# Feed-forward stage, first batch: statistics and normalising of the next x tile by tile over seven steps, turning and copies a step later

## The reference

```python
x = x + tanh(g_xattn) * cross_attention(layernorm(x), ctx)      # x: 16 batches of 512 x 512, f32
h = layernorm(x) @ W1 + b1                                      # 512 -> 2048
imag = w_imag * sin(phases + 0.1 * h)
q = h + (cos(phases) * w_real + sin(phases) * w_imag) * imag * 0.1
x = x + tanh(g_ffn) * (relu(q) @ W2 + b2)                       # 2048 -> 512
```

## Time and profile before

| | |
|---|---|
| median of 3 runs | 2136.64 us (2135.77 to 2136.66) |
| the profiled execution's own time | 2137.62 us |
| its span | 2135.8 us |
| PE busy | 2112.7 us (99%) |
| DVE, ACT, POOL busy | 1436.0 (67%), 1163.2 (54%), 398.5 us (19%) |
| mean granted TensorE clock | 0.998 |

### The profile page before, as it was taken

The page is one execution under the profiler, slowest core; times in us unless marked ns, Lnnn a source line. Parts: engine busy times, 40 slices in busy tenths (PEclk is TensorE's granted clock), DMA queues, the critical chain, the costliest instruction groups (busy, mean ns, idle before and its releaser), DMA issues.

```text
span 2135.8 us, 29046 instructions
## 1 busy us (share of the span) xinstructions
PE 2112.7 (99%) x10331; PEld 1709.8 (80%) x10331; DVE 1436.0 (67%) x2457; ACT 1163.2 (54%) x3463; POOL 398.5 (19%) x324
## 2 busy tenths in 40 slices
PE   9999999999999999999999999999999999999999
PEld 7777777777777778888888888888888888888887
DVE  5587778778776587666665666656666666566654
ACT  3487777777777465444444444444454444544443
POOL 3043443344443311010110100101101011010110
PEclk9999999999999999999999999999999999999999
DMA  7644444454453351231222312213123122231210
GB/s 237 153 115 117 128 114 121 124 117 116 127 120 98 130 137 60 60 79 60 40 72 47 79 60 60 66 42 70 60 60 79 60 40 66 53 79 59 40 40 21
DMA packets 372491, 181.88 MB, mean 85 GB/s; under 512 B 294390, under 2 KB 308954, under 8 KB 372346
## 3 DMA queue, kind: packets, MB, share of 16 engines
q1 hardware_dynamic: 371274, 179.52, 33.1%
q0 software_dynamic: 640, 0.47, 0.1%
q10 hardware_dynamic: 432, 0.04, 0.0%
HBM read 106.34 MB, written 56.85 MB: 76 GB/s over the span
## 4 chain that ended last, share of the span: by engine, by line
PE 64%; DVE 1%; ACT 0%; issue 0%; ACTq 0%; DVEq 0%
PE pair_bank L56 32%; PE m_bank L56 32%; DVE w_split L1474 0%; DVE hidden L1508 0%; DVE turns L1504 0%; DVE sine L1501 0%; ACT relu L1434 0%; ACT hidden L1443 0%; ACT turns L1445 0%; DVE stats L181 0%; DVE relu L1491 0%; DVE x_in L206 0%; ACT sine L1450 0%; DVE residual L1516 0%; DVE mean L191 0%
## 5 line engine op out<-in xcount | busy, mean ns | idle before, releaser
L56 PE MATMUL pair_bank<-w_split,relu 128*128 128x512 f32 x3072 | 738.3, 389 | 3.9 <-DVE relu L1491 3.2
L56 PE MATMUL m_bank<-xT,w_split 128*128 128x512 f32 x3024 | 726.3, 389 | 0.0
L56 PEld LDWEIGHTS pair_bank<-w_split,relu 128*128 128x128 f32 x3072 | 576.1, 188 | 125.4 <-issue 3.6
L56 PEld LDWEIGHTS m_bank<-xT,w_split 128*128 128x128 f32 x3024 | 567.6, 188 | 117.9
L1450 ACT ACTIVATE sine<-turns 128x512 f32<-128x512 f32 x256 | 161.8, 632 | 393.5 <-DVE turns L1504 393.5
L947 ACT ACTIVATE exps<-pair_bank,lowest 128x77 f32<-128x77 f32 x1024 | 316.7, 348 | 62.7 <-DVE lowest L1116 62.5
L1434 ACT ACTIVATE relu<-hidden 128x512 fp32r<-128x512 f32 x256 | 161.9, 632 | 331.4 <-PE m_bank L56 232.1
L1491 DVE SCALAR_TENSOR_TENSOR relu<-hidden,relu 128x512 fp32r<-128x512 f32 x256 | 181.2, 708 | 202.4 <-ACT relu L1434 202.4
L1508 DVE SCALAR_TENSOR_TENSOR hidden<-sine,sine_gain,hidden 128x512 f32<-128x512 f32 x256 | 197.0, 769 | 169.9 <-ACT sine L1450 169.9
L201 POOL TENSOR_TENSOR rstd<-var_eps,minus_half 128x4 f32<-128x4 f32 x32 | 38.2, 1194 | 1156.7 <-DVE var_eps L197 1156.7
L947 ACT ACTIVATION_READ_ACCUMULATOR exps<-pair_bank,lowest 128x1 f32 x1024 | 235.1, 230 | 0.0
(11 more groups left out here) (136 smaller groups left out, 1711.9 us busy)
## 6 DMA issues: line engine op xcount, KB each, us to landing
residual<-in_x_dram SPq DMA_DIRECT2D x64, 256.0 KB, 2.7
x_scratch<-residual SPq DMA_DIRECT2D x64, 256.0 KB, 2.1
x_in<-x_scratch SPq DMA_DIRECT2D x16, 1024.0 KB, 5.6
residual<-x_scratch SPq DMA_DIRECT2D x64, 256.0 KB, 3.3
out_dram<-residual SPq DMA_DIRECT2D x64, 256.0 KB, 2.1
quad_scratch<-x_in SPq DMA_DIRECT2D x60, 256.0 KB, 4.8
x_in<-quad_scratch SPq DMA_DIRECT2D x60, 256.0 KB, 4.4
x_in<-in_x_dram SPq DMA_DIRECT2D x8, 1024.0 KB, 6.5
```

The source lines that it names most:

```text
L56: mm = pe.matmul(out, stationary(s), moving(m), start=first and n == 0, stop=last and n == len(PASSES) - 1)
```

## The change

For batch 0 alone: `sums` does one tile at the end of each of the steps 1 to 4 in place of all four at step 2; `statistics` moves from step 2 to step 5; `normalise` does two tiles at the end of step 6 and two at step 7 in place of four at step 4; turning moves from steps 9 and 10 to 10 and 11; the copies from 11 and 12 to 12 and 13. On SP the regrouping moves from before the load of chunk 10 to before that of chunk 12. The other batches are as before, and no instruction is added or removed; the waits that `sums` and `normalise` begin with are issued once per call.

```diff
@@ sync
                 for n in range(STAGED, CHUNKS):
-                    if n == NORM_AT + 2 * STAGED:
+                    if n == NORM_AT + 2 * STAGED + 2:
                         regroup_x(1)
                     sp.wait_ge(chunk_split, n - STAGED + 1)
                     load_chunk(sp, n)
@@ scalar, batch
                         step(b, f)
-                        if f - AHEAD in XT_AT and not last:
-                            x_hi(b + 1, 1 - slot, XT_AT[f - AHEAD])
+                        late = 1 if b == 0 else 0
+                        if f - late - AHEAD in XT_AT and not last:
+                            x_hi(b + 1, 1 - slot, XT_AT[f - late - AHEAD])
@@ vector, batch
                         step(b, f)
-                        if not last:
+                        if b == 0:
+                            if 1 <= f < 1 + NT:
+                                sums(dve, B + 2, x_in, (f - 1,))
+                            if f == 1 + NT:
+                                statistics(dve, B + 2)
+                            if f in (2 + NT, 3 + NT):
+                                normalise(dve, B + 2, x_in, range(f % 2 * HALF, (f % 2 + 1) * HALF))
+                        elif not last:
                             if f == LN_AT:
...
-                            if f in TURN_AT:
-                                x_turn(b + 1, TURN_AT[f])
-                            if f - AHEAD in XT_AT:
-                                x_lo(b + 1, 1 - slot, XT_AT[f - AHEAD])
+                        if not last:
+                            late = 1 if b == 0 else 0
+                            if f - late in TURN_AT:
+                                x_turn(b + 1, TURN_AT[f - late])
+                            if f - late - AHEAD in XT_AT:
+                                x_lo(b + 1, 1 - slot, XT_AT[f - late - AHEAD])
```

## The result

The median is 2141.23 us (2139.37 to 2143.49, 12 runs) against 2136.3 us (2134.9 to 2138.8, 12 runs) of the kernel before: 1.002 times, 95% interval 1.0013 to 1.0028, so slower by 0.2%, 4.9 us. The profiled execution took 2141.39 us, its span 2139.6 us, 3.8 us over that of before. The forecast was 2140.1 us, in a range from 2136.4 to 2142.2.

A forecast was written before the change was run, and what follows sets the result against it. PE was taken to bound the kernel, busy 2112.7 us. A gain of 3.5, a loss of 5.0 at the regrouping and 2.0 by the clock made 2136.64 + 3.5 = 2140.1 us; range 2136.4 to 2142.2 us for 8 in 10.

The forecast's parts named there:

- The gain, 3.50 us: PE in steps 2 to 4 of the feed-forward stage's first batch no longer waits for `relu_lo`, winning 3.50 us.
- The adds, 3.7 us: POOL's four adds now meet DVE in steps 6 and 7 and delay it 3.7 us, bounds 2.1 and 4.2.
- The regrouping, 17.4 us and three steps: From normalising's end to chunk 12 take 17.4 us, with three steps left instead of four; PE 5.0 us late in step 10.
- The clock, 2 us: PE's clock falls to 1.2 GHz behind the stop before step 10's second product, costing 2 us, between nothing and 3.4.
- The sum: Whole kernel: - 3.5 + 5.0 + 2.0 = + 3.5 us, 0.16% slower.
- Rival 1: PE's clock behind the stop stays low as long as in the attention stage, costing 3.4 us: + 4.9 us; chance 0.25.
- The range: Whole kernel, for 8 in 10: 2136.4 to 2142.2 us, from - 0.2 to + 5.6.
- Rival 2: PE's stop before step 10's second product is there but the clock stays full: + 1.5 us; chance 0.20.
- Rival 3: Chunk 12 reaches ACT in time, so the change keeps its 3.5 us: 2133.1 us; chance 0.10.
- Rival 4: DVE's row statistics in steps 1 to 4 are not hidden, normalising ends 2.4 us later: + 5.9 us; chance 0.05.

The follow-up runs named there:

- the adds late: The changed kernel, but POOL's four residual adds of batch 0 wait until the last tile is normalised; 2136.97 us, 1.0001 times the kernel before.
- the filler experiment: The changed kernel with 18 more products, into a PSUM bank nothing reads, on PE in step 10 before its wait; 2138.96 us, 1.0011 times the kernel before.
- chunk 12 first: The changed kernel with the regrouping before chunk 13, turning and copies one more step later; 2134.93 us, 0.999 times the kernel before.
- In halves: The changed kernel, SP storing batch 0's first two tiles behind step 6, the others behind step 7; 2135.84 us, 0.9993 times the kernel before.

## Why the prediction was right, by its steps

- **The gain, 3.50 us:** right to the hundredth. The bare cycle of 4.87 us held with a row statistic in each (r(1) to r(2): 4.86), as did the seven small instructions at step 5.
- **The adds, 3.7 us:** the last normalising ended at 780.32, forecast 780.5, and counted from s(1) it ended 3.7 us later than in the run with the adds late. By its parts it was not quite as told: all four adds met a busy DVE and cost 1.07, 1.09, 1.03 and 0.97 us, 4.2 in sum, the upper bound; half a microsecond came back, since the rounding behind them had no longer to wait for ACT. What I missed is that all four fall into step 6 and come in one piece before s(6): I expected them in steps 6 and 7 and checked s(7) alone, and s(6) was 0.75 us late. The Trainium skill, SBUF — State Buffer, section "Who interferes with whom", has a mechanism for it, a lock for a whole instruction. The four instructions agree with it in kind; in size they lost about 1.04 us each, not the adds' 1.73 each on POOL (6.92 us for four in this trace), so the rows and not the rule gave the sum. That the adds were the cause is shown (with the adds late the first pair of normalisings took 1.00 us, not 1.97); that it was by this lock is not.
- **The regrouping, 17.4 us and three steps:** right, the term that decides, and 0.8 us too short. It took 18.2 us here (780.32 to 798.48), of which the stores and their landing 10.0 in place of 9.1. With the adds late it took 18.5 us (777.14 to 795.60), and there the stores took 9.2 us and the loads and the chunk longer. What makes this microsecond is not settled. From ACT's start on the chunk to s(10) were 4.9 us, forecast 5.0. So s(10) was 5.69 us late where 5.0 were forecast.
- **The clock, 2 us:** it fell, and cost 1.74 us. The 2 us were a choice between nothing and 3.4 us, so that they came so near is partly luck; that the clock would fall was argued from a row. Without the filler experiment this would be only a coincidence in time; with it, it is shown. The Trainium skill, TensorE: Matmul & The Clock Gate, section "HAM oscillation — how this bites in real kernels", was right that products behind a DMA wait of this kind run at the lower clock, and the trace agrees (0.64 of the clock over 803.4 to 808.2, where the fall itself came 0.6 us behind the start of the products).
- **The sum:** + 3.5 forecast, + 3.9 in the trace (s(10) 0.7 more, the clock 0.3 less: the two misses partly cancel), + 4.9 at the median. Rival 1 (the clock low for longer, + 4.9) fits the median, but neither trace of the change shows it; the interval of the ratio, 2.8 to 6.0 us, holds the 3.9 too. The profiled execution of before stood 1.3 us over its median of 2136.3 and that of the change 0.2 over its own, and the traces differ ahead of s(1) by up to 3.5 us for other reasons; whether the other microsecond is of that kind stays open.
- **The range:** the bounds as worked out, + 1.5 - 1.6 and + 4.9 + 0.5, give - 0.1 and + 5.4, not - 0.2 and + 5.6; the result lies inside either. That a difference of under 4.3 us could not be told was too careful: the interval of the twelve runs is 3.2 us wide, from 2.8 to 6.0, and does not reach zero.
- Rivals 2, 3 and 4 are out: the clock did not stay full, chunk 12 did not come in time, and the row statistics were hidden.

## What to carry to other kernels

When work is moved later in a hand-written order, follow its DMAs to whatever stands behind them in the same queue, and count the steps that are left for a time of transit that hardly changes: here 18 us against three steps of 4.9. A gain of 3.5 us on the engine that sets the time was lost to a weight load that has nothing to do with the work that was moved; putting that load ahead in the queue, and moving another engine's adds out of the way, gave the gain back in full.

## What the runs showed of the hardware

- TensorE's clock fell from 2.4 to 1.2 GHz (granted clock 1.00 and 0.50) within 1.3 us behind stops of 2.2, 4.7 and 4.8 us, and in the course of one of 14.2 us, and it stayed at 1.00 behind stops of 0.6, 1.1 and, between the two stages, 1.6 us. Behind each of the four stops 1.7 us were lost, whatever its length.
- In the trace of the change an add of 128x512 f32 on GpSimd beside a busy VectorE cost VectorE 1.0 to 1.1 us, nearly the same for a fraction, a split, hidden and a normalising, though these take from 0.5 to 1.2 us by themselves.
- The regrouping through DRAM, 1 MB out in four stores and back in four loads, needed 9.1 to 10.7 us for the way out. The next chunk's load in the queue was on chip 17.2 to 18.7 us after the last tile was ready, and 19.3 us with another chunk's load issued just ahead (chunk 12 first). In halves the way out behind the last tile was 5.1 us.
